# Attention of a two-layer gated block: the value products of two key tiles put together ahead of every second head

## The reference, cut to what matters

```python
scores = jnp.einsum('bhqd,bhkd->bhqk', q, k) / jnp.sqrt(DH)
scores = scores + relative_bias          # layer 1: + mask * -1e9
attn = jax.nn.softmax(scores, axis=-1)
out = jnp.einsum('bhqk,bhkd->bhqd', attn, v)
```

## Time and profile before

| what | value |
|---|---|
| median of three runs | 996.31 us (994.21 to 996.57) |
| profiled execution, its own time | 998.35 us |
| span of its trace | 996.6 us |
| mean granted clock of TensorE | 0.977 of full |
| attention of layer 0, first score to last normalised result | about 62 to 284 us |
| attention of layer 1 | about 436 to 660 us |
| PE busy | 941.2 us (94%) |
| DVE, ACT, POOL busy | 582.7, 494.1, 572.7 us |

### The profile page before, as it was taken

How to read it: one execution, slowest core, us unless ns; L and a number is a source line. 1 busy time by engine, 2 the same in 40 slices (tenths; PEclk the granted TensorE clock), 3 DMA queues, 4 the chain that set the end, 5 groups by cost and what they waited for, 6 DMA issues and landing times. The chain is left out here.

```text
span 996.6 us, 21412 instructions
## 1 busy us (share of the span) xinstructions
PE 941.2 (94%) x7733; PEld 535.7 (54%) x7734; DVE 582.7 (58%) x1716; ACT 494.1 (50%) x676; POOL 572.7 (57%) x611
## 2 busy tenths in 40 slices
PE   6979999999989999989999999997899999999994
PEld 3544444444467444544444444465456677777753
DVE  4868888888828444568888888837442222222227
ACT  2438778777845233337887778744111122222210
POOL 3449999999957611149999999951046122222210
PEclk9979999999989999979999999999999999999998
DMA  9563837364143332325353524131812112122153
GB/s 304 194 213 63 234 66 223 77 178 102 22 138 100 119 95 67 88 85 118 66 119 65 116 49 106 34 89 51 297 59 85 61 59 63 59 64 64 53 165 109
DMA packets 96910, 107.56 MB, mean 108 GB/s; under 512 B 15690, under 2 KB 80722, under 8 KB 96818
## 3 DMA queue, kind: packets, MB, share of 16 engines
q1 hardware_dynamic: 86498, 88.30, 32.4%
q10 hardware_dynamic: 6912, 8.65, 2.8%
q0 software_dynamic: 3408, 9.38, 2.6%
HBM read 76.92 MB, written 29.38 MB: 107 GB/s over the span
## 5 line engine op out<-in xcount | busy, mean ns | idle before, releaser
L636 ACT ACTIVATE pT<-ps 128x1024 f32<-128x1024 f32 x256 | 248.6, 1023 | 85.8 <-PE ps L510 85.5
L674 POOL TENSOR_TENSOR xT<-nmax,xT 128x512 f32<-128x512 f32 x192 | 195.7, 1041 | 22.4 <-DVE nmax L578 22.3
L674 POOL TENSOR_TENSOR s<-nmax,s 128x512 f32<-128x512 f32 x188 | 192.6, 1041 | 22.4 <-DVE nmax L578 18.1
L578 DVE CUSTOM_DVE_ANT_0 s<-ps,bias 128x512 f32<-128x512 f32 x256 | 166.1, 688 | 41.1 <-PE ps L497 39.9
L578 DVE CUSTOM_DVE_ANT_0 xT<-ps,bias 128x512 f32<-128x512 f32 x256 | 166.5, 689 | 39.2 <-PE ps L497 33.5
L497 PE MATMUL ps<-ks,qs 97*128 97x512 bf16 (+1 forms) x512 | 162.3, 398 | 10.0 <-PEq L156 4.8
L525 PE MATMUL ps<-pT,vq 128*32 128x512 f32 x1024 | 135.1, 604 | 2.5
L1571 POOL DMA_INDIRECT slots_out<-y,id x39 | 38.2, 980 | 130.1 <-DVE y L1898 130.1
L497 PEld LDWEIGHTS ps<-ks,qs 97*128 97x128 bf16 (+1 forms) x512 | 30.7, 98 | 130.3 <-DVE nmax L578 64.5
L1650 PE MATMUL ps<-gu,xgT 128*128 x312 | 98.8, 460 | 0.7 <-ACT xgT L1734 0.7
L510 PEld LDWEIGHTS ps<-ident,xT 64*128 64x128 f32 x2048 | 69.4, 139 | 28.1 <-issue 27.8
(11 more groups left out here) (203 smaller groups left out, 1210.8 us busy)
## 6 DMA issues: line engine op xcount, KB each, us to landing
bias<-in_bias SPq DMA_DIRECT2D x14, 1024.0 KB, 6.0
qk_scratch<-parts SPq DMA_DIRECT2D x64, 128.0 KB
qs<-qk_scratch SPq DMA_DIRECT2D x32, 192.0 KB, 3.3
ks<-qk_scratch SPq DMA_DIRECT2D x32, 192.0 KB, 3.9
gu<-in_gate_up SPq DMA_DIRECT2D x8, 704.0 KB, 9.4
slots_in<-zeros SPq DMA_DIRECT2D x4, 1280.0 KB, 7.5
xg<-slots_in SPq DMA_DIRECT2D x39, 130.0 KB, 2.1
qk_scratch<-parts ACTq DMA_DIRECT2D x32, 128.0 KB
```

The source lines that it names most:

```text
L578: nc.vector.tensor_tensor_reduce(at.s[m % 4][:, qt, :], sb.ps[:, ring_bank(tile_place[u - 1 + hg * 64]), :], at.bias[:, j if per_head_bias ...
L636: nc.scalar.activation(at.pT[:, slot(m // HG, m % HG), 2 * half:2 * half + 2, :], sb.ps[:, 2 + 2 * half:4 + 2 * half, :], ACT.Exp).then_in ...
L674: nc.gpsimd.tensor_tensor(s, at.nmax[:, m % 4, qt:qt + 1].to_broadcast([P, S]), s, ALU.subtract).then_inc(pool_less_max, 1)
```

## The change

`values` of one key tile ahead of each head becomes `values` of two key tiles ahead of each head with odd `j`, and none ahead of the others. Key tiles 0 and 1 stand at `j == 1`, 2 and 3 at `j == 3`. All else keeps its place.

```diff
                 for m in range(M):
                     b, j = m // HG, m % HG
                     ahead = not (last and m + 2 >= M)
-                    if not (first and b == 0):
-                        values(*before(hg, b), j)
+                    if j % 2 and not (first and b == 0):
+                        for kt in (j - 1, j):
+                            values(*before(hg, b), kt)
                     if ahead:
                         scores(hg, m + 2, (0, 1))
                     if j == 0 and not (first and b < 2):
```

## The result

The changed kernel takes 1033.65 us, median of four runs (1030.80 to 1034.63), against 996.02 for the kernel before measured beside it (994.21 to 996.57). The ratio is 1.0379, with a 95% interval of 1.0361 to 1.0398: 37.6 us slower. The forecast was 1033 (1017 to 1044).

The account below looks back on a forecast made before the run. PE was taken as the bound, busy 53.50 of 53.80 us in four batches. Per layer 16.4 + 0.8 + 0.8 + 0.3 = 18.3 us, for two 36.5, added to 996.31: 1033 us, range 1017 to 1044.

Parts of the forecast that it names:

- PE as the bound: Steady attention batches: PE busy 53.50 of 53.80 us, no room, so all stalls lengthen the batch.
- The stall of the fourth score: Heads 0 and 2: fourth score waits 0.52 us for DVE's release of the first's bank; pair of heads +0.45 us.
- turn_out's wait: Head 0: `turn_out` needs the second score's bank, weights load 1.94 us after first score; pair with it +0.81 us.
- The saving of a pair: Heads 1 and 3: two key tiles of values in a row take 1.86 us, 2.00 if no saving.
- ACT's wait at head 0 gone: Head with `turn_out`: the values' 0.14 us wait for ACT's exponentials goes, since no values stand there.
- ACT and POOL not in the way: Attention batches: ACT's copy of bank 6 stays hidden with some 0.6 us to spare; POOL gains room.
- The end of a layer: Last batch, second pair: head 14's turning waits for head 13's exponentials; head 15's turning at 5.19 against 4.88, +0.31 us.
- The sum: Each layer: 16.4 + 0.8 + 0.8 + 0.3 = 18.3 us; both layers 36.5 us, median 1033 us.
- Only the saving stays: Rival: fourth score never waits, 12.6 us less, 983.7 us; chance 4%.
- It evens out: Rival: within 0.3%, by stalls of 0.1 to 0.2 us per pair or another engine pacing the attention; chance 3%.
- The clock falls: Rival: regular PE stalls lower the clock in the attention, 1061 us, or 1176 if it stays down; chance 6%.
- One argument against this rival: Layer 1's first batch: with longer stalls the clock came back up by itself, 0.50 at 446.5, 0.98 from 449.5.

Follow-up runs that it names:

- two experiments that move `turn_out`: Changed kernel with `turn_out` at head 1 instead of head 0: 1023.96 us; changed kernel with `turn_out` between second and third of head 0's four scores: 1023.30 us.
- the first: Changed kernel with the fourth score between the halves of the turning in heads 0 and 2, `turn_out` behind the turning: 998.70 us, ratio 1.0048.
- the next: Kernel before, second new score between the halves of each head's turning from the second batch on, `turn_out` behind the turning: 1021.78 us, ratio 1.0254.
- The later ones: Changed kernel, split turnings also in first batch, `turn_out` at head 1: 997.25 us; kernel before, split in first batch only: 996.56; kernel before, `turn_out` ahead of values: 994.11.

## Why the prediction was right

- **PE as the bound.** Each stall of PE lengthened the batch by itself: busy time per four batches 53.50 before and 53.41 after, stretch 53.80 and 58.76 us.
- **The stall of the fourth score, +0.45 for a pair of heads.** The four scores of heads 0 and 2 behave as those in the first batch, at 1.33 us. Heads 1 and 2 together take 6.86 us (152.36 to 159.22) against 6.89 in the forecast.
- **turn_out's wait, +0.81 with it.** Its matmuls were forecast at 2.05 after the first score and seen at 2.04, the turning at 2.59 in both, the head at 3.74 in both. Only its weight load came later, at 2.00 instead of 1.94, and it is the row of the matmuls that names VectorE, not that of the weight load as was foretold. No row of before showed it; two experiments that move `turn_out` gave 14.20 (forecast 14.22) and 14.37 (14.37).
- **The saving of a pair, 0.14.** 1.86 us, and 0.28 more a batch when it is undone.
- **ACT's wait at head 0 gone, ACT and POOL not in the way.** As forecast in the batches; POOL only waits more. At the end of a layer ACT is in the way, which the next term counts.
- **The end of a layer, +0.31.** Seen +0.37: head 14's turning ends with the exponentials it waits for, as foretold, a little later.
- **The sum.** A batch 14.69 instead of the 14.71 of the terms, and 37.6 us in the medians against 36.5. The traces allow a stricter test. From the `turn_out` of the third batch to the last one of the layer, at the full clock in both kernels, layer 0 takes 207.01 us (93.05 to 300.06) instead of 189.73 (93.37 to 283.10), 17.28 more, and layer 1 17.27 more. The terms for that stretch are 13 x 1.26 for the batches, 4.08 - 3.22 = 0.86 for head 13 and 0.31 for the end: 17.55. So 34.6 us are shown at the full clock, where the terms gave 35.1. That the medians then come within 1.1 us of the forecast is in part luck, since single executions of one kernel spread by some us. The distance in the two spans, 32.4, is smaller, and the profiled execution took 1030.80 where 1034.9 was forecast; the start of layer 1 at the low clock (7 us in one, 13 in the other) is one difference that the terms did not count.
- **The rivals.** Only the saving stays: excluded by the waits for VectorE at the fourth score. It evens out: excluded by the longer batch. The clock falls: once up, it stayed at 1.00 through both attentions (from 69 to 304 us and from 461.7 to 693), with PE idle for 0.3 and 0.5 us at a time in every batch. The Trainium skill (TensorE: Matmul & The Clock Gate, "A second HAM failure mode: psum-queue depth-cycling") tells of a kernel whose clock swings; here a ring of banks with brief regular waits did not bring it down. One argument against this rival was misread: in layer 1's first batch, at the low clock, PE's stalls were not longer. PE was busy for 1.41 to 1.50 of each 1.50 us from 442.0 to 449.5, against 0.98 in 451.0 to 452.5 at the full clock.

What failed were the forecasts of a better kernel. In the first, 0.15 us for a split head and 0.13 for a `turn_out` behind transposes had been left out of the sum; in the next, the price of the split, taken from that run, was too low (0.15 for 0.25 where both scores stand alone). The later ones foretold gains of a few us, which the times did not show.

## What to carry to other kernels

Work that stands between two groups of matmuls may be what covers another engine's release of a bank: before it is gathered elsewhere, walk the ring with the other engine's start (here 0.58 us behind the matmul) and its step (0.61), and see which matmul comes to a bank too early. Gathering like matmuls does save something, but compare the saving (0.14 us) with the wait it lays bare (0.52 and 0.55). A stretch of the same kernel that already has the new order, here the first batch, prices it before anything is run.

## What the runs showed of the hardware

- Values of four heads in four column groups: a second key tile right behind the first costs 0.86 us instead of 1.00.
- Four transposes of `turn_out` behind two scores add 0.45 us, behind a turning 0.58.
- A turning of 32 transposes takes 1.15 us, two halves of 16 with a score between them 0.64 or 0.65 each; a score of 512 columns that stands alone among transposes takes 0.32, in a row 0.27.
- PE's weight load of a score for the freed bank starts 0.75 us after VectorE began its 0.69 us operation on that bank, in the places that I read (76.02 to 76.77 before, 150.35 to 151.10 after). The weight load of `turn_out` came 0.81 behind (150.96 to 151.77).
- With PE idle for 0.3 and 0.5 us at a time in each batch, the granted clock stayed at 1.00 over two stretches of more than 230 us.
